# Two sets of x rows, gathers ahead of scatters, one branch a round, earlier weights and masks in a four-layer expert kernel

## Time and profile before

| what | value |
|---|---|
| median of 3 runs | 1374.97 us (1373.78 to 1380.35) |
| the profiled execution | 1373.17 us |
| its span | 1371.5 us, 27294 instructions |
| PE busy | 1149.1 us (84%) |
| DVE busy | 985.4 us (72%) |
| ACT busy | 649.1 us (47%) |
| POOL busy | 450.9 us (33%) |
| mean granted PE clock | 0.909 |

### The profile page before, as it was taken

The page is one execution under the profiler, slowest core; times in us unless marked ns, Lnnn a source line. Parts: engine busy times, 40 slices in busy tenths (PEclk is TensorE's granted clock), DMA queues, the critical chain, the costliest instruction groups (busy, mean ns, idle before and its releaser), DMA issues.

```text
span 1371.5 us, 27294 instructions
## 1 busy us (share of the span) xinstructions
PE 1149.1 (84%) x8142; PEld 1064.4 (78%) x8142; DVE 985.4 (72%) x1700; ACT 649.1 (47%) x1359; POOL 450.9 (33%) x341
## 2 busy tenths in 40 slices
PE   5788949999999989989964659996569867799997
PEld 3677849989989989989943559996469855688886
DVE  6656877877878878878648567765468757777775
ACT  3433227667667657657333356651247542222231
POOL 4000016566666666566500035630046600000000
PEclk8899979999999999999966769997779978999999
DMA  6200246776876876776320066623067620000001
GB/s 178 77 19 2 78 166 220 226 219 196 230 220 198 234 219 193 234 220 190 75 70 32 31 256 232 240 81 112 31 193 241 177 84 4 23 25 23 23 23 61
DMA packets 72467, 183.56 MB, mean 134 GB/s; under 512 B 14050, under 2 KB 47586, under 8 KB 60130
## 3 DMA queue, kind: packets, MB, share of 16 engines
q1 hardware_dynamic: 50690, 143.34, 30.3%
q0 software_dynamic: 21728, 39.65, 13.6%
HBM read 155.09 MB, written 27.87 MB: 133 GB/s over the span
## 4 chain that ended last, share of the span: by engine, by line
PE 42%; DMA 20%; issue 15%; DVE 15%; POOL 3%; ACT 2%; POOLq 2%; DVEq 1%; SPq 0%; another core or an unknown queue 0%; ACTq 0%
DMA x_rows<-w_raw,slot_rows 14%; PE ps L663 13%; PE ps L664 13%; PE ps L665 13%; DMA x_tok<-z_gate_rows,slot_rows 2%; DVE hidden_lo L1395 2%; DMA y_rows<-w_raw,slot_rows 1%; POOLq L580 1%; DMA scratch<-in_L_w 1%; DVE x_tok L1752 1%; PE ps L787 1%; DVE featA_hi L1601 1%; POOL x_rows L603 1%; DVE w_lo L1395 1%; PE ps L675 1%
## 5 line engine op out<-in xcount | busy, mean ns | idle before, releaser
L1202 ACT ACTIVATE hidden_f<-ps,b_block 128x256 f32<-128x256 f32 x432 | 221.0, 512 | 186.6 <-PE ps L665 154.1
L603 POOL DMA_INDIRECT x_rows<-w_raw,slot_rows x76 | 193.4, 2545 | 160.0 <-DMA x_rows<-w_raw,slot_rows 117.9
L1395 DVE TENSOR_TENSOR hidden_lo<-hidden_f,hidden_hi 128x512 fp32r<-128x512 f32 x300 | 193.6, 687 | 61.9 <-ACT hidden_hi L1231 36.7
L1203 ACT ACTIVATE hidden_hi<-ps,b_block 128x256 fp32r<-128x256 f32 x432 | 222.7, 515 | 0.0
L663 PE MATMUL ps<-w_hi,featA_hi 128*128 128x256 f32 (+1 forms) x624 | 179.4, 288 | 8.2 <-DVE featA_lo L1395 3.5
L664 PE MATMUL ps<-w_lo,featA_hi 128*128 128x256 f32 (+1 forms) x624 | 178.3, 286 | 0.0
L665 PE MATMUL ps<-w_hi,featA_lo 128*128 128x256 f32 (+1 forms) x624 | 178.2, 286 | 0.0
L663 PE MATMUL ps<-featB_hi,hidden_hi 128*128 128x256 f32 x608 | 175.6, 289 | 0.0
L664 PE MATMUL ps<-featB_lo,hidden_hi 128*128 128x256 f32 x608 | 173.2, 285 | 0.0
L665 PE MATMUL ps<-featB_hi,hidden_lo 128*128 128x256 f32 x608 | 171.9, 283 | 0.0
L574 POOL DMA_INDIRECT x_tok<-z_gate_rows,slot_rows x76 | 87.7, 1154 | 200.3 <-DVE slot_rows L1549 161.8
(11 more groups left out here) (378 smaller groups left out, 3137.9 us busy)
## 6 DMA issues: line engine op xcount, KB each, us to landing
z_tok<-in_L_w SPq DMA_DIRECT2D x48, 1024.0 KB
scratch<-in_L_w SPq DMA_DIRECT2D x48, 1024.0 KB
b_block<-in_L_ffn_b POOLq DMA_DIRECT2D x60, 128.0 KB
z_tok<-in_L_w SPq DMA_DIRECT2D x12, 512.0 KB
scratch<-in_L_w SPq DMA_DIRECT2D x12, 512.0 KB
z_rows<-z_tok SPq DMA_DIRECT2D x8, 512.0 KB, 3.0
z_tok<-y_rows SPq DMA_DIRECT2D x8, 512.0 KB, 5.5
w_raw<-in_L_w SPq DMA_DIRECT2D x12, 256.0 KB, 2.7
```

The lines of the kernel that those rows point to most:

```text
L603: gp.indirect_dma_start(XD, bass.IndirectOffsetOnAxis(ap=TOK[:, q * BTT + tt:q * BTT + tt + 1], axis=0), YB[:, k, tt, :], None, compute_op ...
L1202: act.activation(HF[:, f // 2, part], ps, func, bias=b1)
L1203: act.activation(HTh[:, k, f // 2, part], ps, func, bias=b1).then_inc(s_hhi[L], 1)
L1395: return nc.vector.tensor_tensor(out, full, hi.bitcast(F32), ALU.subtract)
```

## The change

1. XD becomes two tensors. XD[0] gets x as it came in, in one DMA of 2 MB early in the first expert, XD[1] gets the gated output of expert 0. `y0_gated` only multiplies (into Z) and no longer adds to X. `scatter_add` of a block adds to XD[k]. It has no wait for the block before and no `s_yb` mark of its own.
2. POOL's order in layer 0 becomes that of layers 1 and 2: gather(i+2, 0), buffer_left(i, 1), scatter(i, 0), bias(i+1, 0), gather(i+2, 1), buffer_left(i+1, 0), scatter(i, 1), bias(i+1, 1). `buffer_left` waits until the scatters of the named buffer have landed and marks `s_yb`.
3. PE, ACT and DVE have one `If(i < steps)` around a whole round, with those for the next round inside it. This holds for the three block layers.
4. The first weights of layer 0's blocks are loaded when the block list is there. W2 of block 1 goes to the second half of X, W1 of block 0 waits until chunk 1 of Z is stored. ACT and DVE split them ahead of x. The one-hots move to other buffers and are made in halves of 8 tiles; `expert_slots(3)` comes between the two parts of the last `output0`; `slot_tokens(0)` comes before the last `y0_gated`; the router splits of layers 1 to 3 come behind the blocks.
5. At the end of layer 0 SP reads both sets back (X and Z), and DVE adds them by `add_back(0)`, tile by tile, before the transposes. The masks of layer 1's pooling, with their own buffer, come right behind the blocks, ahead of the condition split.

```diff
-        XD = nc.dram_tensor("x_rows", [ROWS, D], F32).ap()
+        XD = [nc.dram_tensor(f"x_rows{k}", [ROWS, D], F32).ap() for k in range(2)]
...
-        ZW = [[Zf[:, 0:HALF_], SCf[:, HALF_:]], [SCf[:, 0:HALF_], Zf[:, HALF_:]]]
+        XH = X[:].rearrange("p t d -> p (t d)")[:, HALF_:]
+        ZWL = [[[Zf[:, 0:HALF_], SCf[:, HALF_:]], [SCf[:, 0:HALF_], last]] for last in (XH, Zf[:, HALF_:], Zf[:, HALF_:])]
...
                 def x_rows(c):
                     sp.wait_ge(s_yfree, TPC * (NC + c + 2))
-                    sp.wait_ge(s_out, 16 * c)
-                    sp.dma_start(XD[0:B * SEQ].rearrange("(t p) d -> p t d", p=P)[:, c * TPC:(c + 1) * TPC, :],
-                                 X[:, c * TPC:(c + 1) * TPC, :]).then_inc(s_out, 16)
+                    sp.wait_ge(s_out, 16 * (c + 1))
+                    sp.dma_start(XD[1][0:B * SEQ].rearrange("(t p) d -> p t d", p=P)[:, c * TPC:(c + 1) * TPC, :],
+                                 Z[:, c * TPC:(c + 1) * TPC, :]).then_inc(s_out, 16)
...
                 half_weights(1)
+                for c in range(1, NC):
+                    sp.wait_ge(s_x[c], 16)
+                sp.dma_start(XD[0][0:B * SEQ].rearrange("(t p) d -> p t d", p=P), X[:]).then_inc(s_out, 16)
                 z_rows(2)
...
                     x_rows(0)
-                    x_rows(1)
...
                 if L == 0:
+                    load_w2(0, 0, first[0])
+                    load_w1(0, 1, first[1])
+                    load_w2(0, 1, first[1])
+                    x_rows(1)
+                    sp.wait_ge(s_out, 16 * 3)
                     load_w1(0, 0, first[0])
                     x_rows(2)
-                    sp.wait_ge(s_tok, 1)
-                    load_w1(0, 1, first[1])
                     x_rows(3)
...
-                    sp.dma_start(Z[:, tiles, :] if L else X[:, tiles, :],
-                                 (YD if L else XD)[0:B * SEQ].rearrange("(t p) d -> p t d", p=P)[:, tiles, :]
-                                 ).then_inc(s_x[c], 16)
+                    for rows, dst in ((YD, Z),) if L else ((XD[0], X), (XD[1], Z)):
+                        sp.dma_start(dst[:, tiles, :], rows[0:B * SEQ].rearrange("(t p) d -> p t d", p=P)[:, tiles, :]
+                                     ).then_inc(s_x[c], 16)
...
                 gp.wait_ge(s_yg, BTT * (q + 1))
-                if q:
-                    gp.wait_ge(s_yst[0][1 - k], 16 * BTT * ((q - 1) // 2 + 1))
-                    gp.sem_inc(s_yb[0], 1)
...
-            gp.wait_ge(s_out, 16 * 2)
+            gp.wait_ge(s_out, 16)
             steps = first_rows(0)
+            gp.wait_ge(s_out, 16 * (1 + NC))
             for i in range(STEPS[0]):
-                for k in range(2):
-                    with gp.If(steps > i):
-                        scatter_add(i, k)
+                with gp.If(steps > i):
+                    if i + 2 < STEPS[0]:
+                        with gp.If(steps > i + 2):
+                            gather(0, i + 2, 0)
+                    if i:
+                        buffer_left(0, i, 1)
+                    scatter_add(i, 0)
                     if i + 1 < STEPS[0]:
                         with gp.If(steps > i + 1):
-                            bias(0, i + 1, k)
+                            bias(0, i + 1, 0)
                             if i + 2 < STEPS[0]:
                                 with gp.If(steps > i + 2):
-                                    gather(0, i + 2, k)
+                                    gather(0, i + 2, 1)
+                            buffer_left(0, i + 1, 0)
+                    scatter_add(i, 1)
+                    if i + 1 < STEPS[0]:
+                        with gp.If(steps > i + 1):
+                            bias(0, i + 1, 1)
...
                 with pe.Fori(0, STEPS[L]) as i:
                     with pe.If(i < steps):
                         hidden(i, 1)
-                    with pe.If(i + 1 < steps):
-                        trans(i + 1, 0)
-                    with pe.If(i < steps):
+                        with pe.If(i + 1 < steps):
+                            trans(i + 1, 0)
                         output(i, 0)
-                    with pe.If(i + 1 < steps):
-                        hidden(i + 1, 0)
-                        trans(i + 1, 1)
-                    with pe.If(i < steps):
+                        with pe.If(i + 1 < steps):
+                            hidden(i + 1, 0)
+                            trans(i + 1, 1)
                         output(i, 1)
...
                 output0(u, 0)
+                if u == 2 * NC - 1:
+                    expert_slots(3)
                 output0(u, 1)
-            for e in range(3, 8):
+            for e in range(4, 8):
...
-                act.wait_ge(s_invp, L + 1)
-                weights(0, 0)
+                if L == 0:
+                    weights(0, 0)
+                    act.wait_ge(s_w2raw[0][0], 16)
+                    act.activation(WB2[0][0][:, 0, :], ZWL[0][0][1], ACT.Copy).then_inc(s_w2hi[0], 1)
+                    act.wait_ge(s_invp, 1)
+                    act.wait_ge(s_w1raw[0][1], 16)
+                    act.activation(WB1[0][0][:, 1, :], ZWL[0][1][0], ACT.Copy).then_inc(s_w1hi[0], 1)
...
                 w1_lo(0, 0)
-                x_lo(0, 0)
...
+                if L == 0:
+                    w2_lo(0, 0)
+                    w1_lo(1, 1)
+                    x_lo(0, 0)
...
-                    nc.vector.scalar_tensor_tensor(X[:, n, :], Z[:, n, :], G[:, n, 0:1], X[:, n, :],
-                                                   ALU.mult, ALU.add).then_inc(s_yfree, 1)
+                    nc.vector.tensor_scalar(Z[:, n, :], Z[:, n, :], G[:, n, 0:1], None, ALU.mult).then_inc(s_yfree, 1)
...
             y0_gated(7, 0)
+            slot_tokens(0)
             y0_gated(7, 1)
-            slot_tokens(0)
+            blocks(0)
             for L in range(1, 4):
                 router_split(L)
-            blocks(0)
-
+            own = pool_masks()
...
-            transposes("x1", TAh, TAl)
+            add_back(0, "x1", TAh, TAl)
```

More of the change, by code:

```diff
@@ L316, in build @@
         YC = 2 * TPC
-        ZD_IN = [16 * (4 + NC + 1 + NC * L) for L in SPARSE]
+        ZD_IN = [16 * (5 + NC + 1 + NC * L) for L in SPARSE]
         H0 = [2 * NC * FB, 0, 0]
@@ L467, in block_weights @@
                     load_w1(0, 1, first[1])
-                for k in range(2):
-                    load_w2(0, k, first[k])
+                    for k in range(2):
+                        load_w2(0, k, first[k])
                 with sp.Fori(0, STEPS[L]) as i:
@@ L746, in expert_slots @@
                 for n in range(NT):
-                    if n == 0:
-                        pe.wait_ge(s_inv, 1 + e)
+                    if n % (NT // 2) == 0:
+                        pe.wait_ge(s_inv, 2 * e + n // (NT // 2))
                     out = PS[0:LC, 6, (e - 1) * P:e * P] if e < 5 else PS[0:LC, 7, (e - 5) * P:(e - 4) * P]
-                    last = nc.tensor.matmul(out, OHH0[:, n, e - 1, :], OHL0[e % 2][:, n, :], start=n == 0, stop=n == NT - 1)
+                    last = nc.tensor.matmul(out, OHH0[:, n, e - 1, :], OHL0[e % 2][n // (NT // 2)][:, n % (NT // 2), :], start=n == 0, stop=n == NT - 1)
                 last.then_inc(s_te, 1)
@@ L1212, in blocks @@
                 with act.Fori(0, STEPS[L]) as i:
-                    with act.If(i + 1 < steps):
-                        weights(i + 1, 0)
                     with act.If(i < steps):
+                        with act.If(i + 1 < steps):
+                            weights(i + 1, 0)
                         hidden(i, 1)
-                    with act.If(i + 1 < steps):
-                        xt(i + 1, 0)
-                        weights(i + 1, 1)
-                        hidden(i + 1, 0)
-                        xt(i + 1, 1)
+                        with act.If(i + 1 < steps):
+                            xt(i + 1, 0)
+                            weights(i + 1, 1)
+                            hidden(i + 1, 0)
+                            xt(i + 1, 1)
             def ffn3():
@@ L1542, in slot_tokens @@
                 inv = PS[:, 5, 16 * NT:16 * NT + S] if L else PS[:, 6, 0:S]
-                empty = SC[:, 6, 0:S]
+                empty = SC[:, 6, 0:S] if L else W2r[:, 384:384 + S]
                 dve.wait_ge(s_invp, L + 1)
@@ L1600, in order0 @@
                         dve.wait_ge(s_te, e - 2)
-                    nc.vector.tensor_tensor(OHL0[e % 2], LANE[:].unsqueeze(1).broadcast_to([P, NT, P]),
-                                            SLO0[:, :, e:e + 1].broadcast_to([P, NT, P]), ALU.is_equal).then_inc(s_inv, 1)
+                    for h in range(2):
+                        tiles = slice(h * NT // 2, (h + 1) * NT // 2)
+                        nc.vector.tensor_tensor(OHL0[e % 2][h], LANE[:].unsqueeze(1).broadcast_to([P, NT // 2, P]),
+                                                SLO0[:, tiles, e:e + 1].broadcast_to([P, NT // 2, P]),
```

(2 more changed lines are left out.)

161 lines of the change are left out of this document (84 added, 77 removed).

## The result

The changed kernel takes 1343.53 us in the median of 4 runs (1337.58 to 1345.88), the kernel before 1375.01 us (1373.78 to 1380.35): a ratio of 0.9757, with a 95% interval from 0.9715 to 0.9799. The profiled execution is the fastest of the four, 1337.58 us with a span of 1335.9.

The account below looks back on a forecast made before the run. The prediction took POOL's chain of scatter waits to set the pace in layer 0's blocks, with PE following. Its terms, -6 - 23 - 0.5 + 3 = -26.5, gave 1348.5 us against the median, range 1338 to 1368.

Parts of the forecast that it names:

- The start: Layer 0 up to the first hidden: earlier slot rows (4.05 us) and earlier weights gain 4 to 6.6, taken as -6.0.
- The rounds: Layer 0's block rounds: gathers ahead of scatters let PE lose most of its 27.7 us excess, taken as -23.
- the bound of -27.7: Layer 0's rounds: the largest gain allowed, PE's whole excess over 11.9 us a block for 32 blocks, none kept.
- The step that failed: Layer 0's rounds: 12.05 us scatter intervals when gating end to first scatter (lag) is 3 or more; PE loses 5 us.
- POOL's load: POOL in layer 0's rounds: lag from gating to scatter at least 3.5 us; stretched gathers could make the sum 2 worse.
- lags of 4 to 8: Sign of being right: POOL waits for x_rows landings in layer 0, scatters starting 4 to 8 us after the gating.
- Branches: Layer 0's 8 empty rounds: one branch each saves 8.7 us on DVE; 5.2 by the Trainium skill's 0.108 us.
- Into layer 1: Last gating of layer 0 to layer 1's scans: 39.2 us in place of 36.2, +3, between 0 and +6.
- the -0.5 for layers 1 and 2: Layers 1 and 2: single branches in their 2 and 3 empty rounds save 0.5 us for both together.
- The first: Rival, layer 0's rounds: scatters keep their 12.7 us interval, rounds gain only 6.7, total 1365; chance 0.2.
- the slower one: Rival, layer 0's rounds: gathers delay landings, each interval 13.46 us, +18.4 instead of -27.7, total 1389; chance 0.06.
- The third: Rival, way into layer 1: masks, adds and a slow clock together cost +8, total 1353.5; chance 0.12.

Follow-up runs that it names:

- run 10: Changed kernel with the last three of layer 0's first four weights loaded only when the token list is there: 1342.78 us, ratio 0.9765.
- run 1: Changed kernel with every scatter adding to the first set of rows, the second holding only the first expert's output: 1339.5 us, ratio 0.9751.
- run 4: Kernel before with one edit, the gather of two rounds on put ahead of the scatter and its wait: 1341.58 us, ratio 0.9763.
- run 5: Kernel before with two POOL waits swapped, so the other buffer is freed before the wait for the gating: 1343.1 us, ratio 0.9777.
- run 8: Changed kernel with the old branches on PE, ACT and DVE: 1351.34 us, ratio 0.983.
- run 9: Changed kernel with the masks made at their old place, behind the last lows: 1342.85 us, ratio 0.9775.
- run 12: Changed kernel with one set of rows, nothing added behind the blocks, biases first, masks in pieces in DVE's waits: 1334.69 us, ratio 0.9711.
- run 11: Changed kernel with the first round's two biases asked for ahead of the second pair of gathers, in every block layer: 1345.55 us, ratio 0.9788.
- run 6: The kernel of run 5 with two idle semaphore increments, some 0.5 us, on POOL between gating wait and scatter: 1377.09 us, ratio 1.0026.
- run 7: Kernel before with DVE's weight splits cut to 8 columns in layer 0's rounds, which alters output and later routing: 1409.07 us.
- run 2: Changed kernel, two sets kept, with POOL's old order (wait for the scatter before, scatter, bias, gather): 1350.62 us, ratio 0.984.

## Why the prediction was right, and where it was not

**The forecast**, 1348.5 in 1338 to 1368, holds with 1343.53. The sum said -26.5 for the profiled execution, which gave -35.6 (medians: -31.5). Of the 9.1 us between sum and profile 6.8 lie in the rounds and 3.1 in the way into layer 1 (-0.07 at its first gather, in place of +3); the rest takes back 0.8. That the total came as near as it did is in part the profiled execution, the fastest of the four: the medians lie 5 us from the sum.

**The start**, -6: measured -5.77, and the parts are other than I had them. The slot rows came 5.6 us earlier, not 4.05. The rest should have come between the first gather and the first hidden, and there is next to nothing: 11.02 us in place of 11.20. Nor is the 5.6 sure: the first gather is at 179.40 here, in seven other kernels with the same work up to that point at 179.69 to 181.46, and in the five with the old start at 184.60 to 185.96, so the start is worth 5 in the mean. Without the early weights 1.65 us return (run 10), less than the 3 to 4 that I put down.

**The rounds**, -23: measured -29.8, outside the bound of -27.7. Half of the step was right: in this order two sets free nothing (run 1), moving the gather does it (run 4), and PE then sets the pace. Its pace is 11.84, not 11.9, which is 1.9 us over 32 blocks. That I could have read: the distances between transposes of the kernel before go down to 11.83, not to 11.9. The step that failed is "At lags of 3 or more it takes 12.05: it loses 0.15 x 33 = 5 us on PE". I had read the interval of the scatters as a price of the chain that depends on the lag, and had the right table for it: 13.46 at small lags, 12.05 at large ones. The cause beneath it was another. A scatter that starts just behind the start of DVE's low is stretched, lands late and makes the next one late; later ones catch up, stretched more or less by what they start under, until one is on time again and hits the low. The row of 3.71 against 1.63 said so, and I used it only to worry about the gathers. Sorted by the time that a scatter's two issues take, the same 31 intervals fall apart more than by the lag: 11.77 in the mean for the 12 under 5.2 us, 13.57 for the 19 above. Without that stretch of the first issue the chain fits under 11.84 at a lag of 0.3 (run 5), and with the gather in front at one of 8, and so nothing of the 27.7 was to be kept back.

**POOL's load.** The lag of "at least 0.85 + 2.66 = 3.5 in every block" became 7.6 and 8.3 by turns, since each gather is stretched to 2.88 us in the mean (1.06 before). By the rule of the Trainium skill (SBUF — State Buffer, Who interferes with whom) I had let a gather take "up to 2 us more", and 1.8 came. But the rule as I gave it is that of the two-port mode, and the second gather of each block is held by a low, which has none by that section, so the size was luck in part. Its price in time, 2 us on the sum, did not come, because nobody waits for it. Nor do the waits for landings with lags of 4 to 8 that I named as a sign exist. But POOL is nearly full: of 11.84 us a block it waits for the gate column only 1.3 (40.1 us in the group above, over 31 blocks).

**Branches**: 9.0 on DVE's way out (run 8) against 8.7. The 1.79 for an empty round of the earlier trace rows held, and so did the choice of the trace over the 0.108 of the Trainium skill's page (Advanced Engine Details and Errata, Control Flow Timing): by it 5.2 would have been saved.

**Into layer 1**, +3: the scan came 38.1 us behind the gating, +2.0, made of 9 us from the branches, about 4 from the masks (run 9), and the adding and its reads, which eat both (some 15 by difference): without them and with a third of the masks, run 12 needs 26.7. By layer 1's first gather the 2 us are back, by a higher granted clock in this execution (0.77 and 0.89, as under run 11); in others they are not (109.1 us in run 1, 111.9 in run 11; 106.9 to 108.2 in the kernel before and those of runs 4 to 6). So the term of +3 was right within what one execution can show. From there to the end of the span the two kernels differ by 0.2 us, so the -0.5 for layers 1 and 2 can't be told from nothing.

**The rivals.** The first (interval 12.7 stays) and the slower one (13.46) rest on the same false reading as the failed step, that a landing takes that long by itself (of the 14.8 us from block 8's scatter to the next, 7.1 are its two issues); the first is what run 6 shows when the start is late again. The third (+8 into layer 1) was not seen either: +2 at the scan, and -0.1 to +4 at layer 1's first gather.

## What to carry to other kernels

Where a queue issues indirect DMAs beside another engine's long instructions, look at the length of single issues in the timeline before you take an interval for the price of a chain: one that is twice the other in the same line says what it runs beside. Swapping two waits was worth as much here, within what the medians can tell, as five coordinated changes. And a fix that is right for one stage (biases first) is tried in that stage alone, since the same helper runs in others where something else is late.

## What the hardware showed that I had not expected

- 0.5 us of delay on POOL in each of 38 blocks moved the time from 1343.1 to 1377.1 us (runs 5 and 6).
- One indirect gather takes 0.99 us to issue on POOL beside short DVE instructions and 2.88 in the mean beside the long ones (run 7, changed kernel); where a single low of 2.29 us covers it, it ends 0.8 us behind that low (308.44 against 307.60).
- An indirect scatter that starts under a long DVE instruction ends 1.5 us after that instruction, wherever under it it started; one that starts 0.04 us before it takes its 1.63 (under run 5).
- The same waits can settle sooner or later: run 2, with the buffer freed ahead of the gating, needed ten blocks to find 11.84 and then kept it, run 5 had it by the fifth. The kernel before and run 6, whose on-time scatters hit the low, never did.
- Of the 14.8 us between two scatters 7.1 are the two issues (324.65 to 331.78) and 7.6 what follows until the next one starts. In the 29 waits of this kind that rest is 5.1 to 8.4 us; with two unstretched issues of 1.6 that would make intervals of 8.6 to 11.9, an estimate. What sets the rest stays open; no run measured the landing by itself.
